# The order of TensorE's units in a fused attention kernel: a planner replaced by a table of 108 steps

## The reference, cut to what matters

```python
h = h + attn(layernorm(h))            # per head: softmax(q k^T / 8) v, then head_kernel
h = h + ffn(layernorm(h))             # shared SwiGLU + two of eight experts, weighted
# attn: q, k, v = x @ wq, x @ wk, x @ wv
# ffn:  group = argmax of 2 logits; expert probabilities = softmax of its 4; top 2 kept
```

## Time and profile before

| | us |
|---|---|
| median of 3 runs | 4832.39 |
| lowest, highest | 4829.75, 4833.71 |
| the profiled execution | 4837.85 |
| its span, first to last instruction | 4836.1 |
| mean granted TensorE clock, share of 2.4 GHz | 0.977 |

### The profile page before, as it was taken

The page is one execution under the profiler, slowest core; times in us unless marked ns, Lnnn a source line. Parts: engine busy times, 40 slices in busy tenths (PEclk is TensorE's granted clock), DMA queues, the critical chain, the costliest instruction groups (busy, mean ns, idle before and its releaser), DMA issues.

```text
span 4836.1 us, 93132 instructions
## 1 busy us (share of the span) xinstructions
PE 4547.9 (94%) x26597; PEld 3326.6 (69%) x26597; DVE 3217.2 (67%) x7726; ACT 2300.9 (48%) x5640; POOL 2946.6 (61%) x1803
## 2 busy tenths in 40 slices
PE   5999999999999999999999999999999999999996
PEld 3667767677676776767677676776767767676775
DVE  5557667577675766657576675776757666576754
ACT  2554545445544544545445444455445445444441
POOL 0776666666665666666666665666656666666661
PEclk7999999999999999999999999999999999999998
DMA  2111111101101111111111111011011111111000
GB/s 53 38 37 31 33 29 38 38 24 33 43 24 37 34 29 39 32 30 39 35 27 33 31 36 38 24 33 44 24 37 34 29 38 32 29 39 35 22 20 18
DMA packets 157061, 159.01 MB, mean 33 GB/s; under 512 B 66576, under 2 KB 148359, under 8 KB 156551
## 3 DMA queue, kind: packets, MB, share of 16 engines
q1 hardware_dynamic: 156551, 152.68, 12.9%
HBM read 59.63 MB, written 19.65 MB: 16 GB/s over the span
## 4 chain that ended last, share of the span: by engine, by line
PE 76%; DVE 6%; issue 5%; DMA 5%; ACT 4%; POOL 2%; ACTq 0%; POOLq 0%; SPq 0%; DVEq 0%
PE o_ps L843 22%; PE work L740 12%; PE scores L824 10%; PE scores L826 9%; PE work L799 8%; PE work L732 3%; PE work L783 3%; DVE part_max L993 3%; DMA q_a<-q_b 2%; DMA sums<-inverse_rows 2%; PE work L725 2%; PE work L760 2%; PE work L751 2%; PE work L788 1%; ACT probs L936 1%
## 5 line engine op out<-in xcount | busy, mean ns | idle before, releaser
L1222 POOL TENSOR_TENSOR sums<-sums,probs 128x736 f32<-128x736 f32 (+3 forms) x1344 | 2366.0, 1760 | 926.7 <-ACT probs L936 871.0
L936 ACT ACTIVATE probs<-scores 128x368 f32<-128x368 f32 (+3 forms) x3456 | 1460.7, 475 | 1494.4 <-PE scores L826 1430.8
L993 DVE TENSOR_REDUCE part_max<-work 128x1 f32<-128x368 f32 (+3 forms) x3456 | 1651.8, 530 | 546.9 <-PE work L740 534.9
L824 PE MATMUL scores<-q_a,k_a 128*128 128x368 f32 (+3 forms) x3456 | 1188.2, 344 | 113.4 <-ACT probs L936 62.1
L843 PE MATMUL o_ps<-probs,values 128*64 128x368 f32 (+1 forms) x6912 | 1230.3, 492 | 3.1 <-issue 3.0
L826 PE MATMUL scores<-q_b,k_b 128*128 128x368 f32 (+3 forms) x3456 | 1148.1, 332 | 0.0
L740 PE MATMUL work<-k_a,q_a 128*128 128x368 f32 (+3 forms) x3456 | 930.3, 357 | 29.3 <-DMA q_a<-q_b 25.6
L843 PEld LDWEIGHTS o_ps<-probs,values 128*64 128x64 f32 (+1 forms) x6912 | 455.5, 139 | 541.2 <-issue 439.1
L824 PEld LDWEIGHTS scores<-q_a,k_a 128*128 128x128 f32 (+1 forms) x3456 | 637.2, 184 | 237.8 <-ACT probs L936 122.3
L740 PEld LDWEIGHTS work<-k_a,q_a 128*128 128x128 f32 (+1 forms) x3456 | 587.7, 185 | 260.0 <-issue 218.2
L826 PEld LDWEIGHTS scores<-q_b,k_b 128*128 128x128 f32 (+1 forms) x3456 | 640.5, 185 | 17.7
(11 more groups left out here) (183 smaller groups left out, 4499.8 us busy)
## 6 DMA issues: line engine op xcount, KB each, us to landing
sums<-inverse_rows SPq DMA_DIRECT2D x192, 184.0 KB
k_a<-k_a SPq DMA_DIRECT2D x128, 184.0 KB, 2.7
q_a<-q_b SPq DMA_DIRECT2D x128, 184.0 KB, 2.7
k_a<-k_a SPq DMA_DIRECT2D x64, 183.0 KB, 2.7
q_a<-q_b SPq DMA_DIRECT2D x64, 183.0 KB, 2.7
resid_rows<-heads_t SPq DMA_DIRECT2D x16, 576.0 KB, 6.1
h_out<-resid_rows SPq DMA_DIRECT2D x16, 576.0 KB, 8.2
heads_t<-in_pe_table_dram SPq DMA_DIRECT2D x16, 512.0 KB
```

The lines of the kernel that those rows point to most:

```text
L824: nc.tensor.matmul(o, k_a[p % 2][i][:, t * P:t * P + n], q_a[p % 2][i][:, c0:c0 + cw], start=True, stop=False)
L936: nc.scalar.activation(probs[0:n, slot(s), i, 0:cw], scores[0:n, h % SB, 0:cw], ACT.Exp, scale=DH ** -0.5).then_inc(probs_ready, 1)
L993: nc.vector.tensor_reduce(part_max[0:n, i * IMG + j if j < IMG else 2 * IMG + i, c:c + 1], w[0:n, 0:keys], AX.X, ALU.max).then_inc(drained ...
L1222: nc.gpsimd.tensor_tensor(acc, acc, probs[0:n, slot(s), :, 0:cw], ALU.add).then_inc(sums_done, 1)
```

## The change

The planner, its costs and `beside_weighing` go. In their place is a table with one entry for each of the 108 steps, between slashes: a letter for each unit in the order in which TensorE does them, and a bar where the value products stand. Every kind of pass reads the same table. Letters of one kind are taken in the order of their chain; where the pass has no such work the letter is dropped, and the bar too where there are no products.

```diff
-PAUSE = ("pause",)
+BURST = ("burst",)
...
-LOAD = {"v": (48, 0, 36), "qk": (48, 95, 130), "max": (16, 50, 0), ...
-SCORE = (66, 0, 70)
-EXCURSION, WEIGH = 25, 62
+TIMETABLE = """
+|kk//k/km|sm/pkmm/pkm/pm|mm/pm/mmpmm/
+|pmmmm/pmm/pmm/mmpm|sm//mmm/m|mm/mmm/mmmmm/
+t|mmmm/tmmm/tmmm/mmm|sm/mg/rvv/|vv/vv/vk/
+|c/kuu/kuu/km|sm/mk/kmuu/m|m/mmmuu/mmmuu/
+|mmm/mmm/mmu/mmm|sm/mmm/mmmu/ummm|m/mmm/mmu/
+mm|m/mmmum/mmu/mm|sm/mmmu/u/vr|v/uuu/uuu/
+u|k/ku/uku/km|sm/kmm/xk/me|mm/e/mmm/
+|m/mmmuu/mmm/mm|smm/mmmm/mummm/m|mmm/fm/mfmuumm/
+m|mf/mmmm/mmm/mm|sm/mmmmu/u/r|v/vvvvuu/vvvvu/
+k|/ku/kuuu/km|sm/km/muku/m|m/mmu/mmmm/
+|mmm/mmmuu/mmmm/ms|m/mmm/ummm/m|mm/mmmum/mum/
+|mmm/mmmu/mmm/mms|mmm/m/r/|//
+""".split("/")
...
 def plan(attn, post, prep):
-    at = [[] for _ in range(ALL)]
...
+    chains = {
+        "k": [(u, of_pair(p)) for p in range(PAIRS) for u in projections((p + 1) % PAIRS)],
+        "m": [(u, of_pair(p)) for p in range(PAIRS) for u in maxima((p + 1) % PAIRS)[0]],
...
+    taken = {letter: iter(chain) for letter, chain in chains.items()}
+    at = []
+    for s, letters in enumerate(TIMETABLE):
         units = []
+        for letter in letters.strip():
+            if letter == "|":
+                if attn and s > 0 or post and s == 0:
+                    units.append(BURST)
+            else:
+                u, wanted = next(taken[letter])
+                if wanted:
+                    units.append(u)
+        at.append(units)
+    return at
...
         def step(seg, it, b, s):
-            units = seg.at[s]
             if seg.attn:
                 score(seg, b, s)
-            if s == 0 and seg.ends:
-                weigh(seg, it, b, 0)
-            if seg.attn and s > 0 and burst(s):
-                early = len(units) // 2 if s % NT else 0
-                for u in units[:early]:
+            for u in seg.at[s]:
+                if u == BURST:
+                    weigh(seg, it, b, s)
+                else:
                     unit(seg, it, b, u)
-                units = units[early:]
-                weigh(seg, it, b, s)
-            for u in units:
-                unit(seg, it, b, u)
```

More of the change, by code:

```diff
@@ L142, in held, with middle @@
     return next(back for back in range(1, ALL) if slot((s - back) % ALL) == slot(s))
-def load(u):
-    return LOAD["upx" if u[0] == "up" and u[2:] == (1, u[3], 1) else u[0]]
+def middle(u):
+    return u[0] == "up" and u[2] == 1 and u[4] == 1
 def plan(attn, post, prep):
-    at = [[] for _ in range(ALL)]
[L151 to L175, removed]
-            for u in units:
[L177 to L229, removed]
-        units = []
[L231 to L237, removed]
@@ L240, in beside_weighing, with of_pair @@
[L240 to L244, removed]
-    return others[:n] + sums + others[n:]
+    ffn = []
+    for c in range(3):
+        ffn += [("up", c, path, k, half) for path in (1, 0) for k in range(KC) for half in range(2)]
+        for t in range(3 * c, 3 * c + 3):
+            ffn += [("shared", t), ("expert", t, 0), ("expert", t, 1)]
+    def of_pair(p):
+        return attn if p < PAIRS - 1 else prep
@@ new lines, in plan @@
+    chains = {
+        "k": [(u, of_pair(p)) for p in range(PAIRS) for u in projections((p + 1) % PAIRS)],
+        "m": [(u, of_pair(p)) for p in range(PAIRS) for u in maxima((p + 1) % PAIRS)[0]],
+        "r": [(("maxrow", (p + 1) % PAIRS), of_pair(p)) for p in range(PAIRS)],
+        "v": [(("v", 1, j), attn) for j in range(NT)] + [(("v", 0, j), prep) for j in range(NT)],
+        "s": [(("sum", PAIRS * NC - 1), post)] + [(("sum", q), attn) for q in range(PAIRS * NC - 1)],
+        "p": [(("proj", j), post) for j in range(NT)],
+        "t": [(("turn2", g), post) for g in range(3)],
+        "g": [(("gate",), post)],
+        "c": [(("count",), post)],
+        "u": [(u, post) for u in ffn],
+        "x": [(("turnx",), prep)],
+        "e": [(("embed", g), prep) for g in range(2)],
+        "f": [(("turn1", g), prep) for g in range(3)]}
@@ L261, in __init__ @@
             for u in units:
+                if u == BURST:
+                    continue
                 k = n % LANES
@@ L945, in step @@
             for u in seg.at[s]:
-                unit(seg, it, b, u)
+                if u != BURST:
+                    unit(seg, it, b, u)
             if seg.post and TURN - 2 <= s <= TURN:
@@ L951, in step @@
             for u in seg.at[s - 1] if s > 0 else []:
-                if load(u) == LOAD["upx"]:
+                if middle(u):
                     wait_drained(act, seg, it, u)
```

8 lines of the change are left out of this document (1 added, 7 removed).

## The result

| | before | after |
|---|---|---|
| median, us | 4831.28 (4 runs) | 4751.91 (4 runs, 4747.33 to 4757.83) |
| ratio, 95% interval | | 0.9836, 0.9819 to 0.9853 |
| profiled execution, its span | 4837.85, 4836.1 | 4757.83, 4756.0 |
| first pass, us | 238.4 | 243.3 |
| one loop pass (of 14) | 292.96 | 286.62 |

The change makes the kernel 79 us faster, 1.6%. The loop wins 6.34 us a pass, 89 us in all; the first and last pass lose 11.

What follows compares the result with a forecast made beforehand. It took TensorE, busy 94% of the span, as the bound, leaving 288 us idle. Terms summed to 2.15 us a pass, 30 us over 14 passes, giving 4802 us; range 4758 to 4834, the forecast's own 4785 to 4820.

Steps and rivals of the forecast that it cites:

- Steps 0 and 1: Loop opening: both projections at step 0 let q's cast start earlier, removing the product's wait; gain 0.9 us a pass.
- Steps 23 to 26: Around the gate: moved value units fill TensorE's wait before step 26; gain 1.4 us a pass, bounds 0.8 and 2.0.
- The turn at step 20: A smaller term for the turn at step 20 of the loop passes: gain 0.2 us a pass.
- The row behind the broadcast: Steps 54 and 81: the row of maxima's DMAs, issued after the slow broadcast, land late; costs 0.8 and 0.6 us a pass.
- The 288 us of idle time are the whole field: Whole kernel: with every matmul kept, the change can only affect TensorE's 288 us idle time and its clock.
- The first and the last pass: Outer passes: longer waits at steps 54 and 81, some 3 and 4 us, eat what these passes win; net 0.
- Banks at 71 to 74: Around steps 71 to 74: fewer maximum products in a row, so fewer bank waits; gain 0.3 us a pass.
- The other projection waits: Steps 30 and 84: reordered units at 29 and 81 remove most projection waits and a bank wait; gain 0.6 us a pass.
- Step 104: Row of maxima: three of the last four products one step earlier shorten its wait for reductions; gain 0.35 us a pass.
- Don't queue behind the broadcast: Rival: the row's DMAs land without waiting behind the broadcast; 2.25 us a pass more won, 4771 or 4762 us; chance 0.12.
- The waits move on: Rival: waits before step 26 and at step 3 reappear at 27 and 2; 4832 to 4828 us; chance 0.12.
- Slower: Rival: late first scores at steps 54 and 81 make the clock fall; 4897 or 4850 us; chance 0.08.

Runs made afterwards that it cites:

- b_open: Kernel before, loop passes only: the k projection of step 1 moved into step 0, step 1 empty; 4810.64 us, ratio 0.9952.
- b_gate: Kernel before, loop passes only: the seven value units of steps 24 and 26 spread over steps 23 to 26; 4825.09 us, ratio 0.9986.
- b_gate2: Kernel before, loop passes only: steps 16 to 26 ordered as in the changed kernel's table, except the k of step 26; 4775.52 us, ratio 0.9888.
- a_mg: Changed kernel with the one maximum product ahead of the gate at step 22 put back behind the sum of step 21; 4751.09 us, ratio 0.9833.
- b_turn: Kernel before, loop passes only: at step 18 the turn stands ahead of the value products instead of behind them; 4829.05 us, ratio 0.9989.
- a_row: Changed kernel with the row of maxima one step earlier, at the end of steps 50 and 77; 4684.38 us, ratio 0.9702.
- a_spread: Changed kernel with the broadcast issued as two DMAs, one for each head's 64 partitions; 4676.91 us, ratio 0.9692.
- a_open: Changed kernel with its opening undone, steps 0 to 3 as in the planner's order; 4788.35 us, ratio 0.9921.
- a_best: Changed kernel with the row of maxima at the end of steps 50 and 77, the broadcast in two DMAs, k before m at step 31; 4673.56 us, ratio 0.9671.
- b_row: Kernel before, loop passes only: the row of maxima one step later, from 50 to 51 and 77 to 78; 4887.65 us, ratio 1.0117.

## Why the prediction was wrong

- **Steps 0 and 1, "I take 0.9".** One of the two terms that failed by most: 2.38 was measured. I priced waits alone, and the net of the waits came to about the 0.9, by luck: not only the product's 0.91 us went but also the 0.58 for ScalarE at the top of step 3, and 1.34 us stand at step 2, where 0.37 stood. What I left out was the clock: 20.5 us at half speed at steps 2 to 4 and 20.5 of the opening went, 1.5 us a pass. The earlier trace rows showed the half clock at step 3; I used it as the price of a rival and not as a gain of the forecast. The first half of this is shown by all seven traces with the new opening, the second by this execution alone; without it the term is about 1.9 (b_open).
- **Steps 23 to 26, "1.4, the middle".** The other: steps 21 to 27 gave 2.89, above my upper bound. The bound was TensorE's wait before step 26; what steps 24 and 27 lost (0.60 and 0.37 us) went for the most part too, and with the wait the slower start of the matmuls behind it. The middle between "work moved" and "whole wait" was no estimate of anything: the moved work without the shorter chain is worth 0.4 us a pass (b_gate), with it and the turns 3.6 (b_gate2). The trace agrees with the rule of the Trainium skill (SBUF — State Buffer, "SBUF: two separate sides"): which of VectorE's operations last 1.0 to 2.1 us changes with the phase, and in pass 8 of the traces looked at (before, after, b_gate, b_gate2, a_mg) each long one of the expert choice ends 0.04 to 0.06 us after one of GpSimd's additions, the long split (2.13 us) 0.41 after.
- **"The turn at step 20, 0.2."** It measured 1.36. I looked at the number of products and overlooked the bar: at step 18 the turn now stands ahead of the value products, and ScalarE's work on it runs under them. b_turn shows this part by itself, 0.8 us.
- **The row behind the broadcast, 0.8 and 0.6.** The mechanism was right, the wait behind the broadcast included (a_row, a_spread); mis-sized were the waits, 2.3 and 1.4 us instead of 1.6 and 0.7, so that both places together cost 2.7 net, with the wait that went at step 50 counted in. The broadcast reaches GpSimd 7.1 us after its issue (2503.73 to 2510.82), not 6.7, and that is 0.4 of the 0.7 missed at step 54. That the row's packets slow it on shared engines would fit, but no view here shows it.
- **"The 288 us of idle time are the whole field."** They were not: of the 80 us that the span lost, 25 are idle time of the page and 55 were in TensorE's busy line, where the half clock stands, and also the slower start behind a wait (the scores at 2373.90 show 0.44 us, those at 2472.18 in a_spread, with no wait, 0.33).
- **The first and the last pass, "0".** They lost 4.9 and 6.3. The long waits that I expected there came, 3.4 and 1.8 us in the first, 2.0 and 4.6 in the last, and what was to be won against them hardly exists in passes that lack half of the units. The last pass took only 274.0 and 274.5 us in a_open and a_mg, whose table differs from the changed kernel's in steps 0 and 1 or 21 and 22; so the 6.3 holds for one pair of executions.
- **Banks at 71 to 74, 0.3:** 1.14. **The other projection waits, 0.6:** 0.46, since the table's steps 31 and 32 wait for banks that the old order did not. **Step 104, 0.35:** 0.38 net; the wait for the maxima itself fell from 0.82 to 0.1.
- **The rivals.** "Don't queue behind the broadcast" is refuted. "The waits move on" describes b_gate and a_best, not the whole. "Slower" had its mechanism right: in b_row the clock fell at step 54 in 12 of 14 passes and the same move cost 56 us. In the table it came in 2 passes of 14. Its condition was too strict: it wanted waits of 3.2 and 2.6 us, and in b_row 2.2 were enough.

Most of the signs of "right" came: the wait of step 3 gone, no wait before step 26 (less than 1 us was asked), waits for q_b at 54 and 81, though of 2.3 and 1.4 us. One came otherwise: I expected one wait for neg_max a pass, and the list has one in the whole kernel. Of the signs of "wrong", two came in part: a gap of 1.34 us before step 2, nearly as large as the 0.58 and 0.91 that went, and half-clock stretches after step 54 in 2 passes. So the mechanisms named were mostly there, and the sizes failed, all towards too little: four gains by 5.0 us a pass together (opening and gate 1.5 each, turns 1.2, banks 0.8), the steps I had called other by 0.7, the row's cost by 1.3, and the outer passes by 11 us in all. That the row's cost was too small too took 1.3 us of the error back, by luck.

## What to carry to other kernels

Write beside every stall the time at half clock that follows it: it is won and lost with the stall, and it can turn up behind another wait that was there all along, so that a single edit measured alone (b_turn, b_open) can show less than its part in a whole. Before pricing a wait behind a slow chain, list everything that stands behind the same chain; the second in line is the next bound. A slow broadcast on few DMA engines holds up what is issued after it; giving it a large outermost dimension took 70 to 75 us off the changed kernel and 25 off the one before, and issuing the short urgent transfer first took 65 to 68 off the changed one.

## What the runs showed of the hardware that I had not expected

The same wait does not always cost the clock. At step 54 TensorE waited for the row in four kernels, 2.2 to 2.3 us on the mean; the granted clock then fell to 1.2 GHz in no pass of 14 (a_mg), 2 (the changed kernel), 11 (a_open) and 12 (b_row). Around step 26 it fell in 2 (before) and 8 (b_open) with a wait of 2.04 us in each pass of both. The kernels differ in the length of a pass, 286.3, 286.6, 289.1 and 296.3 us for the first four. Each count is of one execution, and no run here shows what decides it.

Two DMAs of 92 KB, each with 64 as its outermost dimension, took away nearly all of GpSimd's waiting for one of 184 KB with an outermost 2, although SyncE spends 1.10 us on issuing them instead of 0.56.
